# One core of Trainium2: a four-engine transformer block whose written-out step orders are all set anew

## The reference

```python
x = L0_attn_embeddings
mod = (_silu(L0_c) @ L0_wmod).reshape(L0_c.shape[0], 6, 1, -1)
...
h = _layernorm(x, axis=-1) * (1 + ca) + sa
x = x + ga * _L0_attn_ref(h, L0_attn_guidance_trajectories)
h = _layernorm(x, axis=-1) * (1 + cb) + sb
x = x + gb * _L0_ffn_ref(h, L0_ffn_wqkv, ...)
```

## Time and profile before

| | |
|---|---|
| time before, median of 3 runs | 959.38 us (955.57 to 961.75) |
| the profiled execution, span on the core | 957.5 us |
| instructions | 19956 |
| busy share PE, DVE, ACT, POOL | 81%, 70%, 69%, 57% |
| mean granted TensorE clock | 0.962 |

### The profile page before, as it was taken

One profiled execution on the slowest core, in us unless ns is written; L12 is line 12 of the kernel. 1 busy time (PEld: TensorE's weight loads), 2 busy tenths in 40 slices (PEclk: granted clock), 3 DMA queues, 4 the chain that ended last, 5 costly groups with the idle time before them and its releaser, 6 DMA issues.

```text
span 957.5 us, 19956 instructions
## 1 busy us (share of the span) xinstructions
PE 778.8 (81%) x7439; PEld 566.8 (59%) x7439; DVE 665.8 (70%) x1575; ACT 660.0 (69%) x1545; POOL 544.8 (57%) x326
## 2 busy tenths in 40 slices
...
DMA packets 12710, 10.02 MB, mean 10 GB/s; under 512 B 1088, under 2 KB 11720, under 8 KB 12616
## 3 DMA queue, kind: packets, MB, share of 16 engines
...
...
## 4 chain that ended last, share of the span: by engine, by line
PE 34%; DVE 22%; ACT 18%; issue 12%; POOL 12%; DMA 0%; POOLq 0%; SPq 0%; ACTq 0%; DVEq 0%
ACT probs L1040 6%; PE pair L737 6%; POOL roots L1561 5%; PE dense L894 4%; DVE qk L1285 3%; POOL qk L1609 3%; DVE space L1486 3%; PE mixed L783 3%; PE dense L975 2%; DVE neg_max L1307 2%; DVE q_norm L1491 2%; PE dense L858 2%; PE mixed L848 2%; PE dense L859 2%; PE dense L860 2%
## 5 line engine op out<-in xcount | busy, mean ns | idle before, releaser
L1609 POOL TENSOR_TENSOR qk<-space 128x512 f32<-128x512 f32 x128 | 178.8, 1402 | 26.1 <-DVE q_norm L1491 23.0
L1561 POOL TENSOR_TENSOR roots<-powers,minus_half 128x32 f32<-128x32 f32 (+1 forms) x33 | 174.8, 5296 | 17.0 <-DVE powers L1499 16.1
L1040 ACT ACTIVATE probs<-pair,neg_max 128x128 f32<-128x128 f32 x512 | 139.1, 397 | 11.3 <-DVE neg_max L1307 10.7
L975 PE MATMUL dense<-wq_hi,h_hi 128*128 128x512 f32 x192 | 93.6, 488 | 50.1 <-DVE space L1486 24.1
L1606 POOL TENSOR_TENSOR space<-space,tables 128x512 f32<-128x512 f32 x64 | 86.9, 1358 | 58.4 <-ACT space L1167 58.4
L1486 DVE TENSOR_TENSOR space<-dense,tables 128x512 f32<-128x512 f32 x128 | 87.5, 683 | 44.0 <-ACT space L1167 43.7
L1307 DVE TENSOR_REDUCE neg_max<-pair 128x4 f32<-128x512 f32 x128 | 81.3, 682 | 31.5 <-PE pair L822 31.4
L1163 ACT ACTIVATE squares<-dense 128x512 f32<-128x512 f32 x128 | 79.0, 618 | 32.6 <-PE dense L977 32.1
L737 PE MATMUL pair<-eye_s,probs 128*128 128x128 f32 x512 | 77.8, 285 | 24.5 <-ACT probs L1040 24.4
L1491 DVE TENSOR_REDUCE q_norm<-squares 128x8 f32<-128x512 f32 x128 | 86.4, 675 | 0.0
L975 PEld LDWEIGHTS dense<-wq_hi,h_hi 128*128 128x128 f32 x192 | 38.2, 199 | 78.8 <-issue 65.6
...
## 6 DMA issues: line engine op xcount, KB each, us to landing
...
```

Of the source, the lines that this page charges most:

```text
L975: pe.matmul(to[:, :], h_hi[:, rows], wq_hi[:, layer, cols], start=True, stop=False)
L1040: last = act.activation(probs[:, ring, hh, :], banks[m][:, hh * P:(hh + 1) * P], ACT.Exp, bias=neg_max[:, ring, hh:hh + 1], scale=1.0)
L1561: return pool.tensor_tensor(to, of, minus_half[0:of.shape[0], 0:of.shape[-1]], ALU.pow)
L1609: pool.tensor_tensor(qk[s][:, t, m * INNER:(m + 1) * INNER], turned_c[:, t % 2, m, :], turned_s[:, t % 2, m, :], ALU.add).then_inc(added, 1)
```

## The change

The four lists of `ORDER` are written anew for all turns. Each list has the same steps as before (685, 595, 555 and 243), each once; no instruction, buffer, wait or signal is another. As the PSUM banks are given out in the order of the `pe` list, which bank a step gets changes with it. Some words move from the start of one turn's text to the end of the one before (`>`), or the other way (`<`). The lines that the prediction speaks of, of `pe`, then of `dve`, then of `pool`:

```diff
--- before.py
+++ after.py
...
-        3:setup.warm.1 3:setup.warm.2 3:setup.warm.3 3:new.mix 3:new.sum 3:setup.warm.4 3:setup.warm.5
-        3:new.stream 3:setup.warm.6"""),
...
-        2:proj.tile.0.0 2:new.turn 2:proj.tile.0.1 2:proj.tile.0.2 2:proj.tile.1.0 2:proj.tile.1.1
-        2:new.dots 2:proj.tile.1.2 <3:setup.warm.7 2:proj.tile.2.0 <3:setup.rows 2:new.mix 2:proj.tile.2.1
...
-        3:a.out.2 3:a.mix.3 3:a.out.3 >0:a.turn.0 3:a.project 3:ff.norm 3:proj.tile.3.1 3:proj.tile.3.2
-        3:new.mix 3:new.sum >0:a.turn.1 3:ff.up.0 3:ff.up.1 >0:a.score.0 3:ff.up.2 3:ff.down"""),
-        steps("""
-        0:a.score.1 0:ff.stats <3:new.stream <3:store.turn 0:a.flip.0 0:a.mix.0 0:a.flip.1 0:a.mix.1
...
-        3:proj.tile.3.2 3:new.sum >0:a.turn.1 3:a.project 3:ff.up.0 3:ff.up.1 3:ff.up.2 3:ff.down
-        >0:a.score.0 3:new.stream 3:store.turn"""),
-        steps("""
-        0:a.score.1 0:a.flip.0 0:ff.stats 0:a.mix.0 0:a.flip.1 0:a.out.0 0:ff.norm 0:a.mix.1 0:a.turn.2
...
-        1:proj.tile.2.2 1:proj.tile.3.0 1:a.mix.3 1:proj.tile.3.1 1:a.out.2 1:a.out.3 1:a.project 2:a.turn.0
-        2:a.turn.1 2:a.score.0 2:ff.stats 1:proj.tile.3.2 2:a.score.1 2:a.flip.0 2:a.mix.0 2:a.out.0
...
+        3:setup.silu 3:setup.mod 3:new.turn 3:setup.guide 3:new.dots 3:setup.warm.0 3:setup.warm.1
+        3:setup.gate 3:new.mix 3:new.sum 3:setup.warm.2 3:setup.warm.3 3:new.stream >2:new.turn
+        3:setup.warm.4"""),
...
+        2:proj.tile.0.0 2:proj.tile.0.2 2:proj.tile.0.1 2:proj.tile.1.0 2:proj.tile.1.2 2:proj.tile.1.1
+        <3:setup.rows 2:new.dots <3:setup.warm.5 <3:setup.warm.6 2:proj.tile.2.0 2:proj.tile.2.1
...
+        3:new.dots 3:a.flip.2 3:a.flip.3 3:a.mix.2 3:a.mix.3 3:a.out.2 3:a.out.3 >0:a.turn.0 3:ff.norm
+        >0:a.turn.1 3:a.project 3:new.mix 3:proj.tile.3.1 3:proj.tile.3.2 3:new.sum >0:a.score.0 3:ff.up.0
+        3:ff.up.1 3:ff.up.2 3:ff.down >0:a.score.1 >0:ff.stats 3:store.turn 3:new.stream"""),
...
+        3:new.sum 3:a.project 3:ff.up.1 3:ff.up.0 3:ff.up.2 3:ff.down"""),
+        steps("""
+        0:a.score.0 0:a.turn.1 0:ff.stats <3:store.turn 0:a.score.1 0:a.flip.0 0:a.mix.0 <3:new.stream
...
+        1:proj.tile.1.2 1:proj.tile.2.0 1:a.mix.2 1:a.flip.3 1:proj.tile.2.1 1:a.mix.3 1:proj.tile.3.0
+        1:a.out.2 1:proj.tile.3.1 1:a.out.3 1:a.project 2:a.turn.0 2:a.turn.1 2:a.score.0 2:a.score.1
+        1:proj.tile.2.2 2:ff.stats 2:a.flip.0 2:a.mix.0 2:a.flip.1 2:a.mix.1 1:proj.tile.3.2 2:a.out.0
...
-        0:proj.tile.0.1 0:proj.tile.1.0 0:proj.tile.1.1 0:proj.rsqrt.0 0:a.mix.2 0:proj.tile.2.0
-        0:proj.tile.2.1 0:a.mix.3 0:proj.unit.0 0:proj.tile.3.0 0:a.project 0:proj.tile.3.1 0:proj.rsqrt.1
...
-        3:a.mix.3 3:new.dots 3:new.sims 3:proj.tile.3.0 3:new.weights 3:a.project 3:ff.hi 3:proj.tile.3.1
-        3:new.gate 3:new.again 3:ff.up.0 3:ff.up.1 3:new.stream 3:proj.rsqrt.1 3:ff.up.2"""),
-        steps("""
-        0:a.score.0 <3:ff.down 0:a.score.1 <3:store.turn 0:ff.stats 0:a.unit 0:a.mix.0 0:ff.norm 0:a.mix.1
...
-        3:new.gate 3:new.again 3:a.project 3:ff.up.0 3:proj.rsqrt.1 3:new.stream 3:ff.up.1 3:ff.up.2
-        3:ff.down"""),
-        steps("""
-        0:a.score.0 <3:store.turn 0:a.unit 0:a.score.1 0:ff.stats 0:a.mix.0 0:ff.norm 0:ff.hi 0:a.mix.1
...
-        3:proj.unit.0 3:a.score.2 3:a.score.3 3:ff.stats 3:proj.tile.3.0 3:a.mix.2 3:ff.norm 3:proj.tile.3.1
-        3:ff.hi 3:a.mix.3 3:ff.up.0 3:proj.rsqrt.1 3:ff.up.1 >0:a.unit 3:ff.up.2 3:a.project 3:ff.down"""),
-        steps("""
-        0:a.score.0 <3:store.turn 0:a.score.1 0:ff.stats 0:a.mix.0 0:ff.norm 0:ff.hi 0:a.mix.1 0:ff.up.0
...
+        3:proj.rsqrt.1 3:a.project 3:new.gate 3:new.again 3:ff.up.0 3:ff.up.1 3:new.stream 3:ff.up.2
+        >0:a.score.0 3:ff.down >0:a.score.1 3:store.turn"""),
+        steps("""
+        0:ff.stats 0:a.mix.0 0:ff.norm 0:a.unit 0:ff.hi 0:a.mix.1 0:ff.up.0 0:ff.up.1 0:ff.up.2 <3:proj.keep
...
+        3:proj.tile.3.1 3:proj.rsqrt.1 3:ff.hi 3:new.gate 3:new.again 3:ff.up.1 3:ff.up.0 3:new.stream
+        3:ff.up.2 3:a.project 3:ff.down >0:a.score.0 3:store.turn"""),
+        steps("""
+        0:ff.stats 0:a.score.1 0:a.mix.0 0:ff.norm 0:a.unit 0:ff.hi 0:a.mix.1 0:ff.up.1 0:ff.up.0 0:ff.up.2
...
+        3:a.mix.2 3:ff.norm 3:a.mix.3 3:ff.hi 3:proj.tile.3.1 3:proj.rsqrt.1 3:ff.up.0 >0:a.score.0
+        3:ff.up.2 3:ff.up.1 >0:a.unit 3:a.project 3:ff.down >0:a.score.1 3:store.turn"""),
+        steps("""
+        0:ff.stats 0:a.mix.0 <3:proj.keep 0:ff.norm 0:ff.hi 0:a.mix.1 0:ff.up.0 0:ff.up.1 0:ff.up.2
...
-        2:proj.tile.3.1 2:new.again 3:a.rsqrt 3:proj.split 3:proj.tile.0.0 3:proj.tile.0.1 3:proj.tile.1.0
-        3:new.stats 3:proj.rsqrt.0 3:ff.stats 3:new.steps 3:proj.tile.1.1 3:new.dots 3:proj.tile.2.0
-        3:proj.tile.2.1 3:ff.hi 3:proj.tile.3.0 3:proj.tile.3.1 3:new.again"""),
...
-        0:proj.tile.3.1 1:a.rsqrt 1:ff.hi 2:new.stats 1:proj.split 2:new.steps 1:proj.tile.0.0
-        1:proj.tile.0.1 1:proj.tile.1.0 1:proj.tile.1.1 1:proj.rsqrt.0 2:proj.split 1:proj.tile.2.0
-        2:a.rsqrt 1:proj.tile.2.1 1:proj.tile.3.0 1:proj.tile.3.1 2:proj.tile.0.0 2:proj.tile.0.1
-        2:proj.tile.1.0 2:new.dots 2:proj.tile.1.1 2:proj.rsqrt.0 2:ff.stats 2:proj.tile.2.0 2:proj.tile.2.1
-        2:proj.tile.3.0 2:proj.tile.3.1 2:ff.hi 2:new.again 3:a.rsqrt 3:proj.split 3:proj.tile.0.0
-        3:proj.tile.0.1 3:proj.tile.1.0 3:new.stats 3:proj.rsqrt.0 3:new.steps 3:ff.stats 3:proj.tile.1.1
-        3:new.dots 3:proj.tile.2.0 3:proj.tile.2.1 3:proj.tile.3.0 3:ff.hi 3:proj.tile.3.1 3:new.again"""),
...
+        3:proj.tile.1.0 3:new.stats 3:proj.rsqrt.0 3:ff.stats 3:new.steps 3:proj.tile.1.1 3:proj.tile.2.0
+        3:proj.tile.2.1 3:new.dots 3:ff.hi 3:proj.tile.3.0 3:proj.tile.3.1 3:new.again"""),
...
+        1:proj.tile.1.0 1:proj.tile.1.1 1:proj.rsqrt.0 1:proj.tile.2.0 1:proj.tile.2.1 2:proj.split
+        1:proj.tile.3.0 1:proj.tile.3.1 2:a.rsqrt 2:proj.tile.0.0 2:proj.tile.0.1 2:new.dots 2:proj.rsqrt.0
+        2:proj.tile.1.0 2:proj.tile.1.1 2:proj.tile.2.0 2:ff.stats 2:proj.tile.2.1 2:proj.tile.3.0 2:ff.hi
+        2:proj.tile.3.1 2:new.again 3:a.rsqrt 3:proj.split 3:proj.tile.0.0 3:proj.tile.0.1 3:new.stats
+        3:proj.tile.1.0 3:proj.rsqrt.0 3:new.steps 3:ff.stats 3:proj.tile.1.1 3:proj.tile.2.0 3:new.dots
+        3:ff.hi 3:proj.tile.2.1 3:proj.tile.3.0 3:proj.tile.3.1 3:new.again"""),
```

More of the change, by code:

```diff
@@ L233 @@
[L233 to L237 removed]
+        2:proj.split 2:new.turn 2:proj.tile.0.0 2:proj.tile.0.1 2:proj.tile.0.2 2:proj.tile.1.0
@@ L283 @@
-        2:proj.tile.2.0 2:proj.tile.2.1 2:a.score.2 2:a.score.3 2:new.weights 2:proj.unit.0 2:ff.stats
-        2:a.mix.2 2:ff.norm 2:proj.tile.3.0 2:a.mix.3 2:proj.tile.3.1 2:ff.hi 2:new.gate 2:new.again
-        2:ff.up.0 2:new.stream 2:proj.rsqrt.1 2:ff.up.1 2:ff.up.2 2:a.project 2:ff.down 3:proj.split
-        3:a.unit 3:a.score.0 2:store.turn 3:a.score.1 2:proj.keep 3:proj.tile.0.0 3:proj.tile.0.1
-        3:proj.tile.1.0 3:a.mix.0 3:new.stats 3:proj.tile.1.1 3:proj.rsqrt.0 3:new.turn 3:a.mix.1
@@ new lines @@
+        2:a.mix.2 2:proj.tile.2.1 2:ff.norm 2:proj.tile.3.0 2:proj.unit.0 2:a.mix.3 2:proj.tile.3.1
+        2:new.gate 2:ff.hi 2:new.again 2:proj.rsqrt.1 2:new.stream 2:ff.up.0 2:ff.up.1 2:ff.up.2 2:a.project
+        3:a.unit 2:ff.down 3:proj.split 3:a.score.0 2:store.turn 2:proj.keep 3:a.score.1 3:proj.tile.0.0
+        3:proj.tile.0.1 3:proj.tile.1.0 3:a.mix.0 3:proj.tile.1.1 3:new.stats 3:proj.rsqrt.0 3:proj.tile.2.0
+        3:new.turn 3:a.mix.1 3:proj.tile.2.1 3:ff.stats 3:a.score.2 3:ff.norm 3:a.score.3 3:proj.unit.0
```

486 lines of the change are left out of this document (243 added, 243 removed).

## The result

The changed kernel takes 868.03 us (867.13 to 872.53) against 960.04 (955.57 to 961.75) on the same chip: a ratio of 0.908, 95% interval 0.904 to 0.912. It is 92 us faster, where 13 were forecast and 927 us was the low end of the range. The profiled execution has a span of 865.3 us and a mean granted clock of 0.984, in place of 957.5 and 0.962. First the page: busy times, and the chain that ended last (both answer to the earlier trace rows), then the group of the tiles' first products (to the earlier trace rows).

What follows compares the result with a forecast made beforehand. No single engine was taken as the bound: four in-order engines hand small tiles to one another. Terms summing to -13.8 us gave a 943.7 us span, plus 1.9 for 945.6, forecast 946 us; 8-in-10 range 927 to 968.

Steps and rivals of the forecast that it cites:

- (1): POOL's waits in slot 3 of turn 1 and in turn 2, with ready tiles behind: -1 us, from nothing to -4.8.
- (2): Entry to turn 2: ff.norm ahead of DVE's unit multiply makes POOL's root_f shorter, -2.0 us, between 0 and -4.3.
- (3): Entry to turn 3: DVE does ff.stats straight after store.turn, -2.3 us, between 0 and -3.4.
- (4): Entry to turn 4: rsqrt.1 right after tile 3.1 shortens DVE's wait for roots, -2.9 us, between 0 and -4.2.
- (5): V-projection tiles on PE and ACT, net 18 later: -4.7 us, plus -0.9 for one moved into the tail.
- Rival D: Slower: later v tiles hold a PSUM bank until ACT's copy, so q or k tiles wait; 967 to 972 us, chance 0.18.
- (6): The start: moves on PE and DVE oppose each other, warm-up blocks included; 0, between -3 and +3 us.
- (7): New holds, turn 2 slot 3: POOL takes ff.hi ahead of two tile adds; 0, or +3.8 us if PE comes sooner.
- Rival A: Every turn becomes like turn 3, as more holds go than were priced: 934 us, chance 0.20.
- Rival B: The named places are off the path and gains are waited for one step later: 957 us, chance 0.18.
- Rival C: POOL's two-operand operations and DVE's unit multiplies collide more and lengthen each other: +10 us, 956 us, chance 0.10.

Runs made afterwards that it cites:

- e1: Kernel before the change with only the start (to 142 us) in the new order: 939.03 us, ratio 0.980.
- e2: Kernel before the change with only turn 1 in the new order: 934.08 us, ratio 0.974.
- e3: Kernel before the change with only turn 2 in the new order: 937.92 us, ratio 0.978.
- e4: Changed kernel with turn 3 and the tail put back in the old order: 889.08 us, ratio 0.930 to the kernel before.
- e5: Kernel before the change with three steps moved on POOL's list alone, behind ready tile adds: 960.36 us, ratio 1.004.
- e6: Changed kernel with POOL's whole old list put back, the other three lists new: 917.78 us, ratio 0.959 to the kernel before.
- e14: Kernel before the change, three POOL roots moved behind tile adds so none runs beside DVE's new.sims: 950.15 us, ratio 0.992.
- e15: Changed kernel, POOL's adds at three places moved to run beside DVE's new.sims: 878.84 us, ratio 0.919 to the kernel before.
- e13: Changed kernel with 336 further pairs of steps swapped where the replay ended sooner: 883.71 us, ratio 0.922 to the kernel before.

## Why the prediction was wrong

The step that failed is the one that says what order could give back: "the 15 us by which turn 2 is slower than turn 3", with the rest of PE's 179 us of idle time left to a few named places, since "the effects are local". That the gain lies in every stretch is shown (e1 to e4; PE's idle time fell by 61 us in all). Why small moves do so much is argued: a mean move of 1.3 places is small for one step, but each lets the other engines' lists move with it, and the waits are passed on among four in-order programs. Turn 3 was no floor, only a third sample of the same kind of order: it fell to 195 us. The sum also took PE's busy 778.8 us as fixed, without a reason, and 31 us of them went. So the sum was 14 us for 92.

A reading of the earlier trace rows was wrong too. In turn 2 PE idled longer than in turn 3 (37.7 and 31.7 us), but not longer than in turn 1 (39.8), where it had 97 fewer instructions to take; the turns were not quite the same work. The sign that the forecast named for being wrong, PE idle near 179 us, did not come: it idled 117.5.

- **(1) POOL's holds**: -1 foretold, +4 measured for the three alone (e5). The term was right as a term and misled as a view of POOL. With the other lists of after, POOL's list is worth 5.1 points (e6). POOL's idle time before root_n and root_f fell by 49 us (143.6 to 94.4), where some 20 were foretold. To ask who waits for the ready work behind a wait isn't enough: one has to ask whether the stretch's chain runs through that engine, and in slots 1 and 2 of turn 2 it did. That isn't enough either, as e5 shows.
- **(2), (3), (4) the entries**: each happened as told (root_f at 1.01, ff.stats behind store.turn, 0.35 us for roots). Their own worth wasn't measured.
- **(5) the v tiles**: -5.6 foretold; alone they cost 3.3 points in the old lists, and taken back 6.4 points in the new. No price of its own can be given to them: it depends on the other lists. The signs foretold came: PE's idle time before attention's transposes of probs fell from 24.4 to 11.9 us, ACT's before v_cross from 12.8 to 2.9. Rival D was right on its mechanism and wrong on its condition: in the new lists the q or k tiles waited 4.0 us for a v copy, where they had waited 7.8.
- **(6) the start**: 0 foretold within 3 us either way, 2.0 points measured (e1), the worst mis-sized single term. In the trace of before eleven windows of 5 us up to 130 us have a granted clock under 0.9 (the expectations say seven, which was miscounted), and they were averaged away in "0.96 to 0.98"; the start has no row of its own in the earlier trace rows.
- **(7)**: 0, as told, by little. At that place after, PE released ACT's product, which began at 508.68; POOL's last add had ended at 505.37 + 2.95 = 508.32.
- **Rival A** had the right idea (more holds go than I priced) and the wrong limit, 934; its "on top, 7" is 2.3 + 2.9 + 0.9 = 6.1. **Rival B** fell. **Rival C**, contention, had the right mechanism with the wrong sign and the wrong victims: I counted POOL's long operations, and the cost lay in DVE's 128x4 steps on the new unit's chain, which the new order takes out of the adds' way.

Together: the replay gives 66 us to order alone, e14 and e15 some 8 to 10 to contention. Some 16 to 18 us are then left for the clock, whose bound is 22.6 and whose estimate by the runs is 12. The replay is an estimate and e13 shows its limit; that the clock fills the rest is argued and not shown.
